# A graph attention and mixture-of-experts kernel: half of the fourth column group of P is split into two f16 halves, and the weight subtraction waits for the masked scores

## The reference, cut to what matters

```
Wh = layernorm(x) @ W
e = leaky_relu(Wh @ a[:256] [:, None] + Wh @ a[256:] [None, :], 0.2)
P = softmax(where((adj > 0) | eye, e, -9e15), axis=1)
x = x + P @ Wh
x = x + ffn(layernorm(x))   # router, 2 of 8 experts per row: 256 -> 1024 -> 256, exact gelu
```

## Time and profile before

| | |
|---|---|
| median of 3 runs | 1002.15 us |
| profiled execution, its own time | 998.11 us |
| its span | 996.3 us |
| PE busy | 951.3 us (95%) |
| DVE busy | 786.8 us (79%) |
| ACT busy | 614.0 us (62%) |
| POOL busy | 635.1 us (64%) |

### The profile page before, as it was taken

One profiled execution on the slowest core, in us unless ns is written; L12 is line 12 of the kernel. 1 busy time (PEld: TensorE's weight loads), 2 busy tenths in 40 slices (PEclk: granted clock), 3 DMA queues, 4 the chain that ended last, 5 costly groups with the idle time before them and its releaser, 6 DMA issues. The chain is left out here.

```text
span 996.3 us, 22957 instructions
## 1 busy us (share of the span) xinstructions
PE 951.3 (95%) x7550; PEld 800.4 (80%) x7551; DVE 786.8 (79%) x1210; ACT 614.0 (62%) x900; POOL 635.1 (64%) x632
## 2 busy tenths in 40 slices
PE   4998999999999999999999999999999999999994
PEld 3887999888888989899888977777777777777762
DVE  7688998999999999999999536788666666567653
ACT  3788988888787888888787453433433433333441
POOL 5312242176575676868728458888888888888652
PEclk9998999999999999999999999999999999999998
DMA  8557878869787697877887886443333332232321
GB/s 274 104 158 197 292 241 242 251 183 295 227 259 245 186 268 263 253 246 225 256 282 203 326 340 226 83 123 62 58 55 49 48 58 42 42 51 46 44 34 22
DMA packets 92236, 170.97 MB, mean 172 GB/s; under 512 B 19952, under 2 KB 69360, under 8 KB 83824
## 3 DMA queue, kind: packets, MB, share of 16 engines
q1 hardware_dynamic: 58384, 134.07, 40.2%
q0 software_dynamic: 24048, 26.23, 17.2%
q10 hardware_dynamic: 9712, 9.45, 3.3%
HBM read 136.91 MB, written 41.19 MB: 179 GB/s over the span
## 5 line engine op out<-in xcount | busy, mean ns | idle before, releaser
L1117 ACT ACTIVATE hf<-tp,b_cols 128x256 f32<-128x256 f32 (+1 forms) x312 | 116.2, 459 | 175.9 <-PE tp L882 167.9
L774 PE MATMUL acc<-wh,pt_hi 128*128 128x256 f16 x768 | 209.9, 273 | 0.0
L775 PE MATMUL acc<-wh,pt_hi 128*128 128x256 f16 x768 | 209.9, 273 | 0.0
L776 PE MATMUL acc<-wh,pt_lo 128*128 128x256 f16 x768 | 209.9, 273 | 0.0
L552 POOL TENSOR_TENSOR x_late<-x_late,wsp 128x1024 f32<-128x1024 f32 x32 | 79.8, 2494 | 171.8 <-DMA x_late<-in_L_ffn_W 166.6
L898 PE MATMUL acc<-w_sb,h_hi 128*128 x568 | 170.9, 379 | 5.0 <-issue 3.7
L1266 DVE SCALAR_TENSOR_TENSOR sc<-t_row,s_col 128x2048 f32<-128x2048 f32 x64 | 166.2, 2597 | 11.6 <-PE tp L755 9.7
L658 POOL DMA_INDIRECT out<-y_sb,yidx x71 | 121.6, 1713 | 65.1 <-DVE y_sb L1589 34.4
L880 PE MATMUL tp<-x_hi,w_sb 128*128 128x256 f16 (+1 forms) x624 | 161.2, 264 | 1.9 <-ACT hf L1117 1.8
L882 PE MATMUL tp<-x_down,w_sb 128*128 128x256 f16 (+1 forms) x624 | 161.2, 264 | 0.0
L881 PE MATMUL tp<-x_lo,w_sb 128*128 128x256 f16 (+1 forms) x624 | 160.8, 263 | 0.0
(11 more groups left out here) (240 smaller groups left out, 1788.4 us busy)
## 6 DMA issues: line engine op xcount, KB each, us to landing
adj_sb<-in_adj SPq DMA_DIRECT2D x64, 1024.0 KB, 6.6
x_late<-in_L_ffn_W SPq DMA_DIRECT2D x32, 512.0 KB, 9.7
wsplit_dram<-wsp SPq DMA_DIRECT2D x32, 512.0 KB, 7.5
w_sb<-wsplit_dram SPq DMA_DIRECT2D x32, 512.0 KB, 8.9
xs<-rows_dram ACTq DMA_DIRECT2D x32, 260.0 KB, 3.1
wsp<-in_L_ffn_W POOLq DMA_DIRECT2D x32, 256.0 KB, 4.8
x<-in_x SPq DMA_DIRECT2D x32, 128.0 KB, 9.7
out<-x SPq DMA_DIRECT2D x32, 128.0 KB
```

The costliest lines, as they stand in the source:

```text
L774: pe.matmul(o, pt_hi[g][:, cols], wh[:, j, 0, :], start=(j == 0), stop=False)
L775: pe.matmul(o, pt_hi[g][:, cols], wh[:, j, 1, :], start=False, stop=False)
L776: m = pe.matmul(o, pt_lo[g][:, cols], wh[:, j, 0, :], start=False, stop=False)
```

## The change

Half of group 3, 4 of its 8 blocks, is split like groups 0 to 2. ACT now runs two instructions for the group, one of 512 columns to f16 (`pt_hi3`) and one of 512 columns in f32 (`pt32`). DVE gets a new instruction, `p_lo_half`, at the end of `attend(i)`. PE takes 12 f16 matmuls and 4 f32 ones in group 3 in place of 8 f32 ones, and its transposes of group 1 of the next tile wait for `p_lo_half`, as it reads `tp1`. In the setup two more pairs of `Wh` get a low half (`wh_lo`).

POOL runs `w_rest(i)` in place of `w_rest(i + 1)` in `attend(i)`, after `row_scales` and after `cast_w(i + 1)` (before: `cast_w(i + 2)`), and with a new wait for `s_b`, that is until `masked(i + 1)` is done. ACT runs `w_scaled(i - 1)` in place of `w_scaled(i)`, and the last one after the first two `scaled` of the expert stage.

```
-            def w_rest(e, q):
+            def w_rest(n):
+                e, q = n // CHUNKS, n % CHUNKS
                 pool.wait_ge(s_wf[q], 16 * e + 16)
                 pool.wait_ge(s_wc[q], 16 * e + 16)
+                pool.wait_ge(s_b, min(n + 2, T))
                 pool.tensor_tensor(wf[q], wf[q], wsp[q][:, 0:CW], ALU.subtract).then_inc(s_wp, 1)
...
-                if i + 1 < T:
-                    w_rest((i + 1) // CHUNKS, (i + 1) % CHUNKS)
                 if i % RB == 0 and in_batch(i // RB - 1):
                     row_scales(i // RB - 1)
-                if i + 2 < T:
-                    cast_w((i + 2) // CHUNKS, (i + 2) % CHUNKS)
+                if i + 1 < T:
+                    cast_w((i + 1) // CHUNKS, (i + 1) % CHUNKS)
+                w_rest(i)
...
                 if g == 1 and i > 0:
                     pe.wait_ge(s_hi, G * i)
+                    pe.wait_ge(s_lo3, i)
...
+                    if j < TW:
+                        hi, lo = (pt_hi[g], pt_lo[g]) if g < GS else (pt_hi3, pt_lo3)
+                        pe.matmul(o, hi[:, cols], wh[:, j, 0, :], start=(j == 0), stop=False)
+                        pe.matmul(o, hi[:, cols], wh[:, j, 1, :], start=False, stop=False)
+                        m = pe.matmul(o, lo[:, cols], wh[:, j, 0, :], start=False, stop=False)
                     else:
-                        m = pe.matmul(o, pt32[:, cols], wh32[:, c, :], start=False, stop=(c == GJ - 1))
+                        m = pe.matmul(o, pt32[:, (c - HJ) * P:(c - HJ + 1) * P], wh32[:, c - HJ, :], start=False, stop=(c == GJ - 1))
...
+                else:
+                    act.activation(pt_hi3[:, :], tp[g % 2][:, 0:HW], ACT.Copy, scale=PSCALE).then_inc(s_hi3, 1)
+                    act.activation(pt32[:, :], tp[g % 2][:, HW:GW], ACT.Copy, scale=PSCALE).then_inc(s_hi, 1)
...
-                    w_scaled(i)
+                    if i > 0:
+                        w_scaled(i - 1)
...
+            def p_lo_half(i):
+                dve.wait_ge(s_hi3, i + 1)
+                dve.scalar_tensor_tensor(out=pt_lo3[:, :], in0=tp[GS % 2][:, 0:HW], scalar=PSCALE, in1=pt_hi3[:, :],
+                                         op0=ALU.mult, op1=ALU.subtract).then_inc(s_lo3, 1)
...
                 if i + 2 < T:
                     scores(i + 2, u, 1)
+                if now:
+                    p_lo_half(i)
```

More of the change, by code:

```diff
@@ L62, in build @@
     TS = GS * GJ
+    HJ = GJ // 2
+    HW = GW // 2
+    TW = TS + HJ
     XC = 8
@@ L123, in build @@
         sc = [sb(f"sc{u}", [P, N], F32, front) for u in range(2)]
-        wh = sb("wh", [P, TS, 2, D], F16, front)
-        wh32 = sb("wh32", [P, GJ, D], F32, front)
+        wh = sb("wh", [P, TW, 2, D], F16, front)
+        wh32 = sb("wh32", [P, GJ - HJ, D], F32, front)
         pt_hi = [sb(f"pt_hi{g}", [P, GW], F16, front) for g in range(GS)]
         pt_lo = [sb(f"pt_lo{g}", [P, GW], F16, front) for g in range(GS)]
-        pt32 = sb("pt32", [P, GW], F32, front)
+        pt_hi3 = sb("pt_hi3", [P, HW], F16, front)
+        pt_lo3 = sb("pt_lo3", [P, HW], F16, front)
+        pt32 = sb("pt32", [P, HW], F32, front)
         x_late = sb("x_late", [P, N], F32, front)
@@ L181, in build @@
         xnt_pair += [b[:, :].bitcast(F32) for b in pt_hi + pt_lo]
-        late_pairs = [0, 1, 2, 3, 12, 13, 10, 11, 4, 5, 14, 15, 6, 7, 8, 9]
-        lows = [p < 2 * TS // 4 for p in late_pairs]
+        late_pairs = [0, 1, 2, 3, 14, 15, 10, 11, 4, 5, 12, 13, 6, 7, 8, 9]
+        lows = [p < TW // 2 for p in late_pairs]
         side = (xt_ps, rt_ps)
@@ L265, in build @@
         s_lo = sem("p_lo_done")
+        s_hi3 = sem("p_hi_of_half_group_done")
+        s_lo3 = sem("p_lo_of_half_group_done")
         s_av = sem("av_done")
@@ L764, in av @@
                     pe.wait_ge(s_hi, G * i + G)
+                    pe.wait_ge(s_lo3, i + 1)
                 if g == 0 and within(i, 2, T):
@@ L767, in av @@
                 if g == 1 and i == 0:
-                    pe.wait_ge(s_whl, TS)
+                    pe.wait_ge(s_whl, TW)
                     pe.wait_ge(s_whh, T)
@@ L959, in wh_of @@
             def wh_of(n):
-                return wh32[:, n - TS:n - TS + 2, :] if n >= TS else wh[:, n:n + 2, 0, :]
+                return wh32[:, n - TW:n - TW + 2, :] if n >= TW else wh[:, n:n + 2, 0, :]
             def wh_hi(j):
@@ L995, in p_hi @@
                     act.wait_ge(s_av, G * i + g - 3)
-                dst = pt_hi[g] if g < GS else pt32
-                act.activation(dst[:, :], tp[g % 2][:, :], ACT.Copy, scale=PSCALE).then_inc(s_hi, 1)
+                if g < GS:
+                    act.activation(pt_hi[g][:, :], tp[g % 2][:, :], ACT.Copy, scale=PSCALE).then_inc(s_hi, 1)
+                else:
+                    act.activation(pt_hi3[:, :], tp[g % 2][:, 0:HW], ACT.Copy, scale=PSCALE).then_inc(s_hi3, 1)
+                    act.activation(pt32[:, :], tp[g % 2][:, HW:GW], ACT.Copy, scale=PSCALE).then_inc(s_hi, 1)
             def normalise(b, k):
@@ L1122, in _ @@
             scaled(1)
+            w_scaled(T - 1)
             act.wait_ge(s_wsp, T)
@@ L1469, in _ @@
             masked(1, 1)
-            for j in range(12, NP - 1):
+            for j in range(10, NP - 1):
                 wh_lo(j)
```

2 lines of the change are left out of this document (removed).

## The result

| | before | after |
|---|---|---|
| median of 6 runs each | 1000.68 us (996.25 to 1003.34) | 1032.75 us (1031.12 to 1035.56) |
| profiled execution, its own time | 998.11 us | 1035.56 us |
| span | 996.3 us | 1033.8 us |
| mean granted clock of TensorE | 0.992 | 0.978 |

The ratio is 1.0345, with a 95% interval of 1.0319 to 1.037. The forecast was 997.6 us, its range 987 to 1004. The change costs 32 us where I expected a gain of 4.6 us.

The account below looks back on a forecast made before the run. PE was taken to set the pace in early tiles, with DVE's stalls behind POOL adding time later. Groups -3.4, early tiles -1.0, last tiles -0.9, ends +0.5 and +0.2 gave -4.6 us: 997.6 us, range 987 to 1004.

Parts of the forecast that it names:

- the stall term: DVE's stalls beside POOL's subtraction in a group of four tiles: taken as 0.7 us, between bounds 0 and 4.7.
- tile A: Tile of a group where DVE waits 1.36 us for a late `p_hi` of group 2; foretold at 15.84 us.
- the walk: Tile-by-tile sum for a group of four after the change, from `masked` to `masked`, without subtraction stalls: 63.1 us.
- upper bound: Most that stalls could cost a group: 4.7 us, what three of its tiles lose now (1.99 + 1.9 + 0.8).
- tile D: Tile just before tile A, where POOL's row scales end with `masked` of tile A; foretold at 15.26 us.
- rival 4: PE's wait dominates: PE and DVE in lockstep add latency to every tile; counted with rival 3, together 0.17.
- rival 3: Slower: `w_rest` holds the first `scores` or precedes `masked`; 2.5 us stalls a group, 1008 us; 0.17 with rival 4.
- tiles A and B: First two tiles of the walk, where rival 3 placed its stalls; 15.84 and 15.8 us, PE's router in the second.
- An early tile: Tile near the start, where PE sets the pace: from 14.80 to 14.48 us, -1.0 us over three.
- The step into the expert stage: Last `w_scaled`, store and release of the first expert: +0.2 us; over 1 us would show the prediction wrong.
- the slower of the two: DVE's plain tile grows by 0.60 to 14.48 us, above PE's 14.38; 19 us at the most over 32 tiles.
- tiles C and D: Last two tiles of a group in the walk, foretold at 16.17 and 15.26 us.

Follow-up runs that it names:

- e2: Kernel before with only the move of the weight subtraction and scaling; group 3 stays whole in f32: 999.37 us, ratio 1.0013.
- e7: Changed kernel with `p_lo_half` computing 8 of its 512 columns, the rest staying zero: 1013.3 us, ratio 1.0164.
- e6: Changed kernel with 26 idle f16 matmuls on PE once a batch, ahead of the group 1 transposes where PE stood: 1023.85 us, ratio 1.0267.
- e11: Changed kernel, each subtraction waiting one `masked` more, logits behind the second `p_lo`, `p_lo_half` cut to 8 of 512 columns: 981.23 us, ratio 0.9819.
- e4: Changed kernel, same order and waits, with POOL's subtraction cut to 8 of 1024 columns: 993.92 us, ratio 0.9945.
- e9: Kernel before with the weight work moved, subtraction waiting one `masked` more, logits behind the second `p_lo`, no split: 983.26 us, ratio 0.9837.
- e1: Kernel before with only the split of half of group 3; POOL's and ACT's weight work stays as it was: 1016.79 us, ratio 1.0182.
- e3: Changed kernel with each subtraction waiting for one `masked` more (n + 3 for n + 2): 999.77 us, ratio 1.0004.

## Why the prediction was wrong

**The step that failed is the stall term**: "I take 0.7, as two of four are in step, one falls into the wait of tile A, and only one or a part of one is left." It measured 6.5 us a batch (69.6 less the walk's 63.1), above even my upper bound of 4.7. Three reasons:

1. The term rested on a wait of the kernel before that the change itself takes away. I wrote that in tile D the row scales end with `masked` of tile A, from the earlier trace rows. That held because the last row scale started 0.01 us after `masked`. The same prediction adds 0.60 us to DVE's tile, which lets the row scale through and the subtraction ahead of `masked`. I never put the two together. e2 shows the other side: without the split the row scale is held as before. The hold was fragile: in e7, with 0.08 us of `p_lo_half`, it was already gone.
2. The bound was taken from stalls on `scores` and small instructions. A held `masked` (2.3 us) plus a held `scores` (1.5 us) in one period, 3.8 us in tile A, was outside it. I had the price of one (2.13 us for a subtraction just ahead of `masked`), and let only a part of one happen in four tiles.
3. The stall was treated as a plain sum. It is amplified: the late `p_lo_half` makes PE stand, which is the rival 4 that I had counted with rival 3, and PE goes on at 1.2 GHz (8 to 9 us, e6). Rival 3 was right in kind, with its place (tiles A and B), and far too cheap at 1008 us.

The Trainium skill, "SBUF — State Buffer", section "Who interferes with whom", says that the order of issue decides who blocks. The runs agree that either side can be the one that is held: in the changed kernel `masked` took 6.72 us beside a subtraction of 2.14, in e7 it took 4.48 beside one of 5.61. That the order of issue decides it they do not show, as the recorded starts do not always fit it (see Open). The page spoke against the change, I quoted it so, and gave it too little weight.

**A smaller miss.** I named `scores` as what a subtraction can hold and did not list the other DVE instructions with two SBUF inputs between the two `p_lo`. The logits cost 0.85 us a batch, 5 us in all.

**What held.** An early tile took 14.40 us, with 14.48 foretold. (PE sets it as much as DVE does: in e11 it takes 14.39, and DVE waits 0.46 us for PE in it.) The walk through A to D is within 0.15 us of the usual tile of e4. `p_lo_half` takes 0.60 us between starts (278.69 to 279.29). An instruction with one input in PSUM is not held by the subtraction. The step into the expert stage cost some 0.3 us, under the 1 us allowed: `split_x(1)` waits 4.75 us for the store of the weights at 625.99, and PE's idle time there is 2.16 us in place of 1.83.

**What I also had wrong in sign.** I wrote that DVE becomes the slower of the two and that the added work is paid in full wherever DVE sets the pace, and then let pay for it with vanished stalls. With the subtraction's stalls gone on both sides the split is a loss of 10 to 15 us: four times 0.60 us on DVE a batch against at most four times 0.42 us on PE. What there is to gain lies in the move: as it stands in the change it gains nothing (e2), and with the right `masked` to wait for and the logits behind the second `p_lo` it gains 17 us (e9).

**Open.** The recorded starts do not always tell who has the lock. In the changed kernel the subtraction is recorded 0.28 us after `masked` (279.95 and 279.67) and went first, in e2 1.37 us after it (283.89 and 282.52) and went first, and in e7 0.87 us after it and was held. The last row scale, recorded 0.01 or 0.02 us after `masked`, was held in the kernel before and in e2 and was not in e7. POOL's record may begin late, or a queue of POOL work behind a cast keeps the port; no run here tells these apart. I also did not find why e1 costs 18 us where the split costs 10 to 15 elsewhere, or why a batch of e1 differs from the next in its tiles C and D. From 140 to 560 us the mean of its `scores` is 2.546 us, against 2.638 in the kernel before and 2.345 in e3, so a good part of the old stalls is still in it.

## What to carry to other kernels

Where two engines exclude each other, a wait holds only as long as the distance that it was read from: before adding 0.6 us to one engine, find every place where the other is now held, and ask what runs there when it is not. Release the background work (here POOL's subtraction) from an event that cannot have passed already when its engine comes to it, and list all instructions with the wrong kind of operands in the window that it is given, the small ones too. Work moved from an engine at 14.8 us a tile to one at 13.9 us does not pay once the second has waits of its own.

## What the runs showed of the hardware

A custom DVE instruction with two SBUF inputs and a GpSimd subtraction delay each other, by up to the whole time of the one that holds: `masked` went from 4.42 to 6.72 us beside a subtraction of 2.14. Other GpSimd instructions are held by `masked` too: an indirect transfer took 4.98 us in place of 0.96 (299.60 beside `masked` at 299.31), and a gate of 128 x 4 took 4.38 us. Direct casts on the same queue stayed at 0.56 to 0.87 us beside anything.

After 3.37 us in which PE stood, the granted clock was 0.50 for 5.6 us, with PE busy all the while from 228.34 on; in e6, where PE did matmuls of no use in that gap and stood 0.54 us, it stayed at 1.00. These 26 matmuls a batch, whose result nobody uses, gave back 8.9 us of 1032.75 (7.8 by the ratios).
